# Output projection of attention in three fp32r terms, with wo split once and loaded from ScalarE's queue, and x in natural layout in other buffers

## The chip, the cores and the metric

The kernel runs on one core of a Trainium2 chip. The metric is the device time of one execution in microseconds (us). The kernel before took 2135.66 us as the median of three runs (2130.54 to 2139.39).

## The reference

The input x has 4 batches of 1024 tokens of 512 numbers. One layer of attention with 16 heads of 32 is followed by a mixture of experts; each adds its input and normalises. All is fp32. The change touches only the last two lines of attention:

```
q, k, v = x @ wq.T + bq, x @ wk.T + bk, x @ wv.T + bv        # 16 heads of 32
probs = softmax(q @ k.T / sqrt(32));  ctx = probs @ v          # per head
attn = ctx @ wo.T + bo                                        # ctx: 1024 x 512 per batch
x2 = layernorm(x + attn)                                      # then the expert part reads x2
```

## The kernel before, in words

Every engine has its own instruction list, written out in the code, and the engines meet at semaphores. A list is strictly in order: an instruction that waits holds up all that stands behind it.

**Batches and groups.** Attention goes through the batches b = 0 to 3. A batch has G = 4 groups of HG = 4 heads, a group has two halves of 512 queries (HALF), and a half has 8 steps of 128 keys. So there are 16 steps (STEPS) a group and 64 a batch (`loc`), with 4 slots each. In a step TensorE makes the scores (L625) of the next step, ScalarE their exps into one of three buffers of probabilities (L776), TensorE multiplies with v (L636). GpSimd and VectorE add the probabilities of two steps ("fold", L539 and L888) into `acc`, and TensorE sums them over the keys into `ps_sum` ("row sums", L649). Beside this TensorE makes max products (L603) and the k and q projections of a group two further on (L577) in three terms of fp32r, where VectorE takes the maxima (L860). fp32r is the faster matmul type; a high part and a low part (the rest) of both factors, in three products, replace one fp32 product.

**The spread.** SyncE copies the projected `kq` into `kq_stack` by twelve DMAs of 256 KB for each group ("spread", L342), then a row of negated maxima (L350, four small writes).

**The inversion.** When a half is done, ScalarE evicts ctx and the sums (L784, L791). SyncE gathers the sums into `sum_few` (L361, four small DMAs, "gather"), VectorE takes the reciprocal (L877), SyncE writes it out and broadcasts it into `res` (L367, L371), and GpSimd multiplies ctx with it (L503, "normalise"). An eighth of ctx, 512 columns of one group, is called a ctx part here; there are 8.

**The tail of a batch.** TensorE makes eight v tiles of the next batch (L569; 4 x 3 fp32r matmuls each, low part of wv reloaded by L396 since `wv_lo` shares its place with `probs_mid`), evicted by VectorE with bv (L906). Then come eight output tiles (L666) of 128 tokens: four fp32 matmuls each of ctx with wo, which appear as two instructions each. wo sits in `acc`, loaded by SyncE when the last row sums are done (L410). VectorE adds x with bo (L916), takes mean and variance (L918 to L924), GpSimd makes scale and shift (L515, L518), ScalarE applies them (L795) and SyncE stores the tile (L421). x in natural layout is loaded into `probs_outer` (L413) behind the inversion, and GpSimd adds bo (L510). Four PSUM banks go round (TAIL_RING). The results lie in `res` and `probs_mid`; between them ScalarE makes the first exps of the next batch. In the last batch there are no v tiles, and half of wo is loaded ahead into `stage` (L404).

**The start.** x and the first weights are split into high and low parts, batch 0's k and q of group 0 are projected, wv is split (ScalarE L822, VectorE L937), then v tiles and max products alternate (`prologue`).

## Time and profile before

| | |
|---|---|
| median of three runs | 2135.66 us |
| the profiled execution | 2128.77 us |
| its span | 2127.0 us |
| mean granted clock of TensorE | 0.99 of full speed |
| TensorE busy | 2040.6 us, 96% of the span |
| VectorE busy | 1266.4 us, 60% |
| ScalarE busy | 862.4 us, 41% |
| GpSimd busy | 871.3 us, 41% |

A busy share is an average over stages. Which engine sets the time of a stage is read from its waits: an engine that idles before an instruction has a releaser, named behind `<-`. Matmuls overlap, so the distance of their starts counts and not their duration. SyncE's rows show the time of issue, not of transfer. The inner tails lie at about 356 to 407, 672 to 723 and 988 to 1039 us, the last one at 1277 to 1315 us; what comes after is the expert part.

### The profile page before, as it was taken

The numbers are of one execution on the slowest core, as the hardware profiler recorded it, in microseconds if no ns is written. First come the engines' busy times: TensorE is split into PE (matmuls) and PEld (weight loads), VectorE is DVE, ScalarE is ACT, GpSimd is POOL, SyncE is SP. The second block draws the span as 40 slices with busy tenths as digits, with TensorE's granted clock in tenths as the row PEclk, the third lists the DMA queues.
The fourth block names the chain that finished last, engine by engine and source line by source line (L and its number), as shares of the span: only waits on it lengthen the run. The fifth ranks groups of instructions, "written<-read, shape, count | busy, mean of one in ns | idle before, by whom it ended". The sixth has DMA issues, their size and how long they took to land. (4 is left out here: it accounts for less than half of the span.)

```text
span 2127.0 us, 29932 instructions
## 1 busy us (share of the span) xinstructions
PE 2040.6 (96%) x9636; PEld 1202.1 (57%) x9637; DVE 1266.4 (60%) x2247; ACT 862.4 (41%) x1530; POOL 871.3 (41%) x828
## 2 busy tenths in 40 slices
PE   7999999999999999999999986899999999999997
PEld 5655556555556555556455432578544444446886
DVE  5777775577775677875678843574222222225875
ACT  2266663366663466663466661321111111112332
POOL 2255754455754555753555553400111111114651
PEclk9999999999999999999999998899999999999999
DMA  5322334221434231434231204661222222225752
GB/s 168 70 49 58 96 76 119 85 56 50 101 75 116 84 69 41 103 71 118 82 76 27 66 12 152 215 242 60 89 89 89 89 89 89 89 79 157 227 176 75
DMA packets 94815, 205.90 MB, mean 97 GB/s; under 512 B 24608, under 2 KB 25120, under 8 KB 92256
## 3 DMA queue, kind: packets, MB, share of 16 engines
q1 hardware_dynamic: 83888, 168.90, 27.1%
q0 software_dynamic: 10800, 35.40, 6.1%
q8 instruction: 69, 1.13, 0.2%
q14 instruction: 58, 0.48, 0.1%
HBM read 113.53 MB, written 39.85 MB: 72 GB/s over the span
## 5 line engine op out<-in xcount | busy, mean ns | idle before, releaser
L860 DVE TENSOR_REDUCE max_half<-ps_side 128x1 f32<-128x512 f32 x1024 | 657.9, 682 | 196.2 <-PE ps_side L603 193.4
L776 ACT ACTIVATE probs_outer<-ps_s 128x512 f32<-128x512 f32 x629 | 363.4, 600 | 210.4 <-PE ps_s L625 179.9
L603 PE MATMUL ps_side<-kq_stack 96*128 96x512 f32 x1024 | 409.2, 404 | 3.1 <-DVE max_half L860 2.3
L625 PE MATMUL ps_s<-kq_stack 97*128 97x512 f32 x937 | 397.1, 425 | 5.0 <-ACT probs_outer L776 3.3
L625 PEld LDWEIGHTS ps_s<-kq_stack 97*128 97x128 f32 x937 | 177.4, 189 | 167.1 <-issue 89.1
L1524 PE MATMUL ps_gu<-gu_sb,xT_e 128*128 x568 | 257.7, 596 | 0.7 <-issue 0.5
L1422 POOL DMA_INDIRECT x_g<-x,who_all x71 | 67.5, 951 | 454.7 <-PE ps_t L1514 358.4
L603 PEld LDWEIGHTS ps_side<-kq_stack 96*128 96x128 f32 x1024 | 195.0, 190 | 56.2 <-DVE max_half L860 26.6
L776 ACT ACTIVATE probs_mid<-ps_s 128x512 f32<-128x512 f32 x308 | 177.6, 599 | 116.0 <-PE ps_s L625 101.7
L539 POOL TENSOR_TENSOR acc<-probs_outer,probs_mid 128x512 f32<-128x512 f32 x129 | 163.9, 1296 | 144.7 <-ACT probs_mid L776 144.7
L539 POOL TENSOR_TENSOR acc<-probs_outer 128x512 f32<-128x512 f32 x129 | 163.4, 1291 | 125.6 <-ACT probs_outer L776 125.6
L539 POOL TENSOR_TENSOR acc<-probs_mid,probs_outer 128x512 f32<-128x512 f32 x118 | 149.7, 1293 | 120.7 <-ACT probs_outer L776 120.7
L636 PE MATMUL ps_ctx<-probs_outer,v_sb 128*32 128x512 f32 x1376 | 173.4, 599 | 0.5 <-ACT probs_outer L776 0.5
L1645 ACT ACTIVATE act_g<-ps_gu 128x256 f32<-128x256 f32 x71 | 27.3, 384 | 346.8 <-PE ps_gu L1524 346.8
L1524 PEld LDWEIGHTS ps_gu<-gu_sb,xT_e 128*128 128x128 f32 x568 | 102.3, 190 | 106.5 <-issue 106.2
L1722 DVE TENSOR_TENSOR hid<-act_g,ps_gu 128x256 f32<-128x256 f32 x71 | 29.9, 421 | 221.8 <-ACT act_g L1645 221.8
L649 PE MATMUL ps_sum<-acc,ones 128*32 128x512 f32 x1024 | 133.8, 594 | 11.2 <-DVE acc L888 7.1
L1547 PE MATMUL ps_d<-wd_sb,act_g 128*128 x284 | 133.7, 593 | 0.5 <-DVE act_g L1729 0.5
L577 PE MATMUL ps_side<-x_hi,wkq_hi 128*128 128x512 f32 x256 | 102.7, 401 | 12.3 <-DVE x_lo L931 10.7
L1466 PE MATMUL ps_gu<-sgu_hi,xT_hi 128*128 128x512 f32 x256 | 104.0, 406 | 3.0 <-issue 1.5
L1735 DVE COPY y_t<-ps_d 128x512 f32<-128x512 f32 x71 | 49.1, 692 | 93.4 <-PE ps_d L1547 93.4
L577 PE MATMUL ps_side<-x_lo,wkq_hi 128*128 128x512 f32 x256 | 102.2, 399 | 0.0
(210 smaller groups left out, 3055.2 us busy)
## 6 DMA issues: line engine op xcount, KB each, us to landing
kq_stack<-kq SPq DMA_DIRECT2D x192, 256.0 KB, 5.1
...
res<-inv_rows SPq DMA_DIRECT2D x128, 64.0 KB, 2.0
...
```

What stands on the lines that cost most here:

```text
L539: nc.gpsimd.tensor_tensor(acc[:, h, :], probs(loc - 1, h), probs(loc, h), ALU.add).then_inc(folded, 1)
L577: done = nc.tensor.matmul(bank, w, xs, start=r == 0, stop=r == UNIT - 1)
L603: nc.tensor.matmul(bank, q_stack[par][0:3 * HD, h, t * P:(t + 1) * P], k_stack[par][0:3 * HD, h, half * HALF:(half + 1) * HALF], start=Tru ...
L625: nc.tensor.matmul(out, k_stack[par][0:3 * HD + 1, h, kt * P:(kt + 1) * P], q_stack[par][0:3 * HD + 1, h, half * HALF:(half + 1) * HALF], ...
L636: done = nc.tensor.matmul(ps_ctx[h * HD:(h + 1) * HD, :], v_sb[:, kt, (g * HG + h) * HD:(g * HG + h + 1) * HD], probs(loc, h), start=kt == ...
L649: done = nc.tensor.matmul(ps_sum[h * HD:(h + 1) * HD, :], ones[:], acc[:, h, :], start=kt == FOLD - 1, stop=kt == KT - 1)
L776: nc.scalar.activation(probs(loc, h), score_bank(b, loc * HG + h)[0], ACT.Exp, scale=HD ** -0.5).then_inc(probs_ready, 1)
L860: nc.vector.reduce_max(max_half[:, u // 2, u % 2:u % 2 + 1], bank, AX.X).then_inc(side_free, 1)
L1422: nc.gpsimd.indirect_dma_start(x_g[:, t % 4, :], None, x2, bass.IndirectOffsetOnAxis(ap=who_all[:, t:t + 1].bitcast(U32), axis=0),).then_i ...
L1466: done = nc.tensor.matmul(out, w, m, start=c == 0 and i == 0, stop=c == last_c and i == 2)
L1524: done = nc.tensor.matmul(ps_gu[:, s % 2, :], e_xT[:, s % 2, c, :], gu_sb[:, bass.ds(e, 1), c, :].rearrange("p a n -> p (a n)"), start=c = ...
L1547: done = nc.tensor.matmul(ps_d[:, s % 2, :], e_hT[:, s % 2, c, :], wd_sb[:, bass.ds(e, 1), c, :].rearrange("p a n -> p (a n)"), start=c == ...
```

## The change

**The projection.** An output tile is made of 12 fp32r matmuls: high and low part of ctx with the high part of wo, and the high part of ctx with the low part of wo (new L714 to L717). The high part of ctx is written over `kq`, the low part over ctx itself. ScalarE makes the high parts (`ctx_high`, new L847), VectorE the low ones (`ctx_low`, new L976). Seven of the eight must be there for the first output tile, the eighth for the fifth. In the inner tails ScalarE makes them after the batch, once the spread has landed, and VectorE between its evictions of v; in the last batch seven are made inside the last group.

**wo.** It is loaded once at the start into `acc`, split by GpSimd and kept in DRAM as two halves of 1 MB. In each inner tail ScalarE's queue loads both (new L892) as soon as the row sums are done: into `acc` and into the third buffer of probabilities. In the last batch SyncE loads them in the middle of the batch over `x_hi` and `x_lo`.

**x.** Tiles 0 to 3 are loaded into the first buffer of probabilities, 4 and 5 into `stage`, both ahead of the inversion, 6 and 7 into `res` behind the last normalisation. The results of tiles 0 to 3 lie in `probs_mid`, the others take x's place. GpSimd adds bo to two tiles ahead of the last normalisation. The gather is a function of its own (`few`) and stands in the tail ahead of these loads.

**The start.** TensorE's first v tile waits for wv's low parts one by one, not for all four, and GpSimd waits for all of them before it splits its weights.

```diff
-NORM_AFTER, SPLIT_W_AFTER = (15, 9), 13
+NORM_AFTER, NORM_AFTER_LAST, SPLIT_W_AFTER = (15, 9), 11, 13
+CTX_ORDER = ((0, 0), (1, 0), (2, 0), (0, 1), (1, 1), (2, 1), (3, 0), (3, 1))
+CTX_HIGH_LAST = {10: (0, 1, 2), 12: (3, 4, 5), 14: (6,)}
+CTX_LOW_AFTER_V = {4: (0, 1, 2), 5: (3, 4), 6: (5, 6)}
...
+    wo_kept = nc.dram_tensor("wo_kept", (2, P, C, D), F32, kind="Internal").ap()
...
-        with nc.sbuf_tensor("probs_mid", [P, HG, HALF], F32) as probs_mid:
-            pass
-        wv_lo = sb("wv_lo", [P, C, D], F32R)
-        acc = sb("acc", [P, HG, HALF])
-        wo = acc
+        probs_mid, wv_lo = twin("probs_mid", "wv_lo", [P, HG, HALF])
+        acc, wo_hi = twin("acc", "wo_hi", [P, HG, HALF])
...
         v_sb = sb("v_sb", [P, KT, D])
-        probs_outer = sb("probs_outer", [P, 2, HG, HALF])
+        probs_first = sb("probs_first", [P, HG, HALF])
+        probs_last, wo_lo = twin("probs_last", "wo_lo", [P, HG, HALF])
...
 
-            return probs_mid[:, h, :] if loc % PROBS == 1 else probs_outer[:, loc % PROBS // 2, h, :]
...
+            return (probs_first, probs_mid, probs_last)[loc % PROBS][:, h, :]
+
+        ctx_sb, ctx_lo = twin("ctx_sb", "ctx_lo", [P, G, S])
+        ctx_hi = kq
+        first_wo = [ctx_lo[:, 2 * i:2 * i + 2, :].rearrange("p g (a d) -> p (g a) d", d=D) for i in range(2)]
...
+        def x_of(t):
+
+            return probs_first[:, t, :] if t < 4 else stage[:, t - 4, :] if t < 6 else res[:, t - 6, :]
+
         def res_of(t):
 
-            return probs_mid[:, t - 2, :] if 2 <= t < 6 else res[:, t % 2, :]
+            return probs_mid[:, t, :] if t < 4 else x_of(t)
...
                 if last and g == 1:
-                    sp.wait_ge(w_split, 2 * B * G)
-                    sp.dma_start(stage[:], woT[:, 0:2, :]).then_inc(wo_in, 16)
+                    sp.wait_ge(proj_ready, PROJ * B * G)
+                    sp.sem_inc(passed_sp, 1)
+                    for i, part in enumerate((x_hi, x_lo)):
+                        sp.dma_start(part[:, :, 0:D].bitcast(F32), wo_kept[i]).then_inc(wo_in, 16)
+
+            def load_x_nat(b, i, to):
+                sp.dma_start(to, x[bass.ds(b, 1), 2 * i * P:(2 * i + 2) * P, :].rearrange(
+                    "a (t p) d -> p (a t) d", p=P)).then_inc(xnat_in[i], 16)
 
             def tail(b, last=False):
+                few((b + 1) * G * NHALF - 1)
                 sp.wait_ge(sum_done, (b + 1) * SUMS)
                 sp.sem_inc(passed_sp, 1)
-                first = 2 if last else 0
-                sp.dma_start(wo[:, first:C, :], woT[:, first:C, :]).then_inc(wo_in, 16)
+                for i in range(2):
+                    load_x_nat(b, i, probs_first[:, 2 * i:2 * i + 2, :])
+                sp.wait_ge(w_split, 2 * min(b * G + G + 3, B * G))
+                load_x_nat(b, 2, stage[:])
                 invert((b + 1) * G * NHALF - 1)
-                for i in range(KT // 2):
-                    sp.dma_start(x_nat[:, 2 * i:2 * i + 2, :],
-                                 x[bass.ds(b, 1), 2 * i * P:(2 * i + 2) * P, :].rearrange(
-                                     "a (t p) d -> p (a t) d", p=P)).then_inc(xnat_in[i], 16)
+                sp.wait_ge(ctx_done, (b + 1) * G * NHALF)
+                load_x_nat(b, 3, res[:])
...
+            sp.dma_start(acc[:], woT).then_inc(const_in, 16)
...
-            sp.wait_ge(wv_split, C)
+            sp.wait_ge(part_low, C)
             sp.dma_start(wv_lo_kept, wv_lo[:].bitcast(F32)).then_inc(wv_moved, 16)
+            sp.wait_ge(const_set, WO_MADE)
+            for i in range(2):
+                sp.dma_start(wo_kept[i], first_wo[i].bitcast(F32)).then_inc(wv_moved, 16)
...
+            sp.wait_ge(wv_moved, KEPT)
...
+            pool.wait_ge(part_low, C)
...
             nc.gpsimd.tensor_copy(wkq_hi[:], first_w(1)).then_inc(w_high, 2)
             pool.wait_ge(w_high, 4)
             nc.gpsimd.tensor_tensor(wkq_lo[:], first_w(1), wkq_hi[:].bitcast(F32), ALU.subtract).then_inc(w_split, 2)
+            pool.wait_ge(const_in, CONSTS)
+            pool.wait_ge(w_split, 4)
+            nc.gpsimd.tensor_copy(first_wo[0], acc[:]).then_inc(const_set, 1)
+            pool.wait_ge(const_set, WO_MADE - 1)
+            nc.gpsimd.tensor_tensor(first_wo[1], acc[:], first_wo[0].bitcast(F32), ALU.subtract).then_inc(const_set, 1)
...
-                    if at == NORM_AFTER[0]:
+                    if at == (NORM_AFTER_LAST if last and g == G - 1 else NORM_AFTER[0]):
                         normalise(b, g, 0)
                     if at == SPLIT_W_AFTER and not (last and g > 0):
                         projected(b * G + g + 2)
                         split_w(b * G + g + 3)
                     if (g, at) in X_AFTER and not last:
                         x_low(b + 1, X_AFTER[g, at])
+                add_bo(b, 0)
+                add_bo(b, 1)
                 normalise(b, G - 1, 1)
-                add_bo(b)
+                for t in range(2, KT + 1):
+                    if t < KT:
+                        add_bo(b, t)
+                    scale_and_shift(b, t - 2)
+                scale_and_shift(b, KT - 1)
...
-            def o_tile(u, t, bank, parts):
+            def o_tile(u, b, t, bank, hi, lo):
+                if t % (KT // NHALF) == 0:
+                    pe.wait_ge(part_low, C + b * CTX_PARTS + (CTX_PARTS - 1 if t == 0 else CTX_PARTS))
                 pe.wait_ge(tail_free, u - TAIL_RING + 1)
+                at = slice(t * P, (t + 1) * P)
                 for g in range(G):
-                    done = nc.tensor.matmul(bank, ctx_sb[:, g, t * P:(t + 1) * P], parts[g],
-                                            start=g == 0, stop=g == G - 1)
+                    nc.tensor.matmul(bank, ctx_hi[:, g, at], hi[g], start=g == 0, stop=False)
+                    nc.tensor.matmul(bank, ctx_lo[:, g, at], hi[g], start=False, stop=False)
+                for g in range(G):
+                    done = nc.tensor.matmul(bank, ctx_hi[:, g, at], lo[g], start=False, stop=g == G - 1)
                 done.then_inc(tail_ready, 1)
...
-            pe.wait_ge(wv_split, C)
             pe.wait_ge(const_set, 5)
             for t, c, what in prologue():
                 if what is None:
+                    if t == 0:
+                        pe.wait_ge(part_low, c + 1)
                     v_tile(t, t, ps_s[:, t % RING, :], RING, [c])
...
-                pe.wait_ge(wo_in, 16 * (b + 1))
+                pe.wait_ge(wo_in, 32 * (b + 1))
                 for t in range(KT):
-                    if t % (KT // NHALF) == 0:
-                        pe.wait_ge(ctx_done, (b + 1) * G * NHALF - (t == 0))
-                    o_tile(b * TAIL + 2 * KT + t, t, tail_bank(KT + t),
-                           [wo[:, g, :] for g in range(G)])
+                    o_tile(b * TAIL + 2 * KT + t, b, t, tail_bank(KT + t),
+                           [wo_hi[:, g, :] for g in range(G)], [wo_lo[:, g, :] for g in range(G)])
...
             for t in range(KT):
-                if t % (KT // NHALF) == 0:
-                    pe.wait_ge(ctx_done, (b + 1) * G * NHALF - (t == 0))
-                o_tile(b * TAIL + KT + t, t, tail_bank(t),
-                       [stage[:, 0, :], stage[:, 1, :], wo[:, 2, :], wo[:, 3, :]])
+                o_tile(b * TAIL + KT + t, b, t, tail_bank(t),
+                       [x_hi[:, g, 0:D] for g in range(G)], [x_lo[:, g, 0:D] for g in range(G)])
...
+                    act.wait_ge(x2_out[h], 16 * (b + 1))
...
+            def ctx_high(b, i):
+                g, half = CTX_ORDER[i]
+                if i == 0:
+                    for s in stacked:
+                        act.wait_ge(s, SPREAD * min(b * G + G + 2, B * G))
+                act.wait_ge(ctx_done, b * CTX_PARTS + g * NHALF + half + 1)
+                at = (slice(None), g, slice(half * HALF, (half + 1) * HALF))
+                nc.scalar.activation(ctx_hi[at], ctx_sb[at], ACT.Copy).then_inc(part_high, 1)
...
+                    for i in CTX_HIGH_LAST.get(loc % STEPS, ()) if last and g == G - 1 else ():
+                        ctx_high(b, i)
...
+                act.wait_ge(wv_moved, KEPT)
+                act.wait_ge(sum_done, (b + 1) * SUMS)
+                for i, part in enumerate((wo_hi, wo_lo)):
+                    nc.scalar.dma_start(part[:].bitcast(F32), wo_kept[i]).then_inc(wo_in, 16)
+                for i in range(CTX_PARTS):
+                    ctx_high(b, i)
                 for t in range(KT):
                     norm(b, t)
...
             batch(B - 1, True)
+            ctx_high(B - 1, CTX_PARTS - 1)
             for t in range(KT):
...
+                    for i in CTX_HIGH_LAST.get(loc % STEPS, ()) if last and g == G - 1 else ():
+                        ctx_low(b, i)
+
+            def ctx_low(b, i):
+                g, half = CTX_ORDER[i]
+                at = (slice(None), g, slice(half * HALF, (half + 1) * HALF))
+                dve.wait_ge(part_high, C + b * CTX_PARTS + i + 1)
+                nc.vector.tensor_tensor(ctx_lo[at], ctx_sb[at], ctx_hi[at].bitcast(F32),
+                                        ALU.subtract).then_inc(part_low, 1)
...
                     v_tile(b * TAIL + KT + t, t, tail_bank(t))
                     if t == 2:
                         invert((b + 1) * G * NHALF - 1)
+                    for i in CTX_LOW_AFTER_V.get(t, ()):
+                        ctx_low(b, i)
                 for t in range(KT):
                     o_tile(b * TAIL + 2 * KT + t, b, t, tail_bank(KT + t))
+                    if t == 1:
+                        ctx_low(b, CTX_PARTS - 1)
```

VectorE in an inner tail, before. `max_row` is the last row of maxima, `v_sb` the eviction of a v tile, `inv_few` the reciprocal, the last row the eviction of the first output tile:

```order
L871 CAST max_row<-ps_side 16x128 [waits row_in1,side_ready]
L906 TENSOR_TENSOR v_sb<-ps_side,bv_bc 128x512 [waits tail_ready] x3
L877 RECIPROCAL inv_few<-sum_few 128x16 [waits rows_out,few_in]
L906 TENSOR_TENSOR v_sb<-ps_side,bv_bc 128x512 [waits tail_ready] x5
L916 TENSOR_TENSOR res<-ps_side,probs_outer 128x512 [waits xbias,tail_ready]
```

The same place now:

```order
L936 CAST max_row<-ps_side 16x128 [waits row_in1,side_ready]
L981 TENSOR_TENSOR v_sb<-ps_side,bv_bc 128x512 [waits tail_ready] x3
L942 RECIPROCAL inv_few<-sum_few 128x16 [waits rows_out,few_in]
L981 TENSOR_TENSOR v_sb<-ps_side,bv_bc 128x512 [waits tail_ready] x2
L976 TENSOR_TENSOR ctx_lo<-ctx_sb,kq 128x512 [waits part_high] x3
L981 TENSOR_TENSOR v_sb<-ps_side,bv_bc 128x512 [waits tail_ready]
L976 TENSOR_TENSOR ctx_lo<-ctx_sb,kq 128x512 [waits part_high] x2
L981 TENSOR_TENSOR v_sb<-ps_side,bv_bc 128x512 [waits tail_ready]
L976 TENSOR_TENSOR ctx_lo<-ctx_sb,kq 128x512 [waits part_high] x2
L981 TENSOR_TENSOR v_sb<-ps_side,bv_bc 128x512 [waits tail_ready]
L987 TENSOR_TENSOR probs_mid<-ps_side,probs_first 128x512 [waits xbias,tail_ready]
```

Seven low parts of ctx stand between the reciprocal and the first output tile, in and around the last v evictions.

SyncE's queue in an inner tail, before, from the last two rows of the spread; `kq_stack<-max_row` is the row write, `sum_few` the gather:

```order
L342 DMA kq_stack<-kq 32x2x1024 [waits scores_ready]
L342 DMA kq_stack<-kq 32x2x1024 x2
L350 DMA kq_stack<-max_row 1x4x128 [waits side_free]
L350 DMA kq_stack<-max_row 1x4x128 x3
L410 DMA acc<-woT 128x2048 [waits sum_done]
L361 DMA sum_few<-res 32x1x16 [waits sum_taken]
L361 DMA sum_few<-res 32x1x16 x3
L367 DMA inv_rows<-inv_few 128x16 [waits inverted,ctx_done]
L371 DMA res<-inv_rows 32x512 [waits rows_out]
L371 DMA res<-inv_rows 32x512 x3
L413 DMA probs_outer<-x 128x2x512 x4
```

The same place now:

```order
L363 DMA kq_stack<-kq 32x2x1024 x2
L371 DMA kq_stack<-max_row 1x4x128 [waits side_free]
L371 DMA kq_stack<-max_row 1x4x128 x3
L382 DMA sum_few<-res 32x1x16 [waits sum_taken]
L382 DMA sum_few<-res 32x1x16 x3
L434 DMA probs_first<-x 128x2x512 [waits sum_done]
L434 DMA probs_first<-x 128x2x512
L434 DMA stage<-x 128x2x512 [waits w_split]
L390 DMA inv_rows<-inv_few 128x16 [waits inverted,ctx_done]
L394 DMA res<-inv_rows 32x512 [waits rows_out]
L394 DMA res<-inv_rows 32x512 x3
L434 DMA res<-x 128x2x512 [waits ctx_done]
```

The load of wo is gone from this queue, and three loads of x stand ahead of the inversion's second half.

VectorE in the last group of the last batch now. `acc` is a fold; before, the same folds followed each other without the rows of `ctx_lo`:

```order
L954 TENSOR_TENSOR acc<-probs_last,probs_first 128x512 [waits sum_done,probs_ready]
L954 TENSOR_TENSOR acc<-probs_last,probs_first 128x512 [waits probs_ready]
L976 TENSOR_TENSOR ctx_lo<-ctx_sb,kq 128x512 [waits part_high] x3
L954 TENSOR_TENSOR acc<-probs_mid,probs_last 128x512 [waits sum_done,probs_ready]
L954 TENSOR_TENSOR acc<-probs_mid,probs_last 128x512 [waits probs_ready]
L976 TENSOR_TENSOR ctx_lo<-ctx_sb,kq 128x512 [waits part_high] x3
L954 TENSOR_TENSOR acc<-probs_first,probs_mid 128x512 [waits sum_done,probs_ready]
L954 TENSOR_TENSOR acc<-probs_first,probs_mid 128x512 [waits probs_ready]
L976 TENSOR_TENSOR ctx_lo<-ctx_sb,kq 128x512 [waits part_high]
L954 TENSOR_TENSOR acc<-probs_last,probs_first 128x512 [waits sum_done,probs_ready]
L954 TENSOR_TENSOR acc<-probs_last,probs_first 128x512 [waits probs_ready]
L942 RECIPROCAL inv_few<-sum_few 128x16 [waits rows_out,few_in]
```

Three low parts stand ahead of a pair of folds twice, and one a third time.

## Rows read from the trace of the kernel before

**Rows 1.** Timeline of TensorE, tails of batches 0, 1: start, us, line, tile, [idle<-releaser]

```profile
354.53 1.06 PE L649 MATMUL ps_sum<-acc,ones 128*32 128x512 f32 x8 [0.18 <-DVE acc L888]
...
359.04 0.39 PE L569 MATMUL ps_side<-wv_hi,x_hi 128*128 128x512 f32 x1
...
377.17 0.39 PE L569 MATMUL ps_side<-wv_lo,x_hi 128*128 128x512 f32 x1
...
378.08 17.33 PE L666 MATMUL ps_side<-acc,ctx_sb 128*128 128x512 f32 x40
...
694.04 17.33 PE L666 MATMUL ps_side<-acc,ctx_sb 128*128 128x512 f32 x40
```

**Rows 2.** Timeline of TensorE, last batch's last group and tail

```profile
1258.84 1.06 PE L649 MATMUL ps_sum<-acc,ones 128*32 128x512 f32 x8 [2.20 <-issue]
...
1281.43 3.55 PE L666 MATMUL ps_side<-stage,ctx_sb 128*128 128x512 f32 x4 [3.90 <-DMA acc<-woT]
...
1284.81 1.88 PE L666 MATMUL ps_side<-acc,ctx_sb 128*128 128x512 f32 x4
...
1308.85 1.88 PE L666 MATMUL ps_side<-acc,ctx_sb 128*128 128x512 f32 x4
```

**Rows 3.** Timeline of VectorE: reciprocals in tail 0, in a body, in tail 1

```profile
372.91 0.25 DVE L877 RECIPROCAL inv_few<-sum_few 128x16 f32<-128x16 f32 x1 [7.54 <-DMA sum_few<-res]
...
444.74 0.25 DVE L877 RECIPROCAL inv_few<-sum_few 128x16 f32<-128x16 f32 x1 [0.17 <-DMA sum_few<-res]
...
690.14 0.25 DVE L877 RECIPROCAL inv_few<-sum_few 128x16 f32<-128x16 f32 x1 [8.81 <-DMA sum_few<-res]
```

**Rows 4.** Timeline of SyncE's queue (SPq): us is the time of issue

```profile
25.41 14.10 SPq L342 DMA_DIRECT2D kq_stack<-kq  x12
...
349.39 14.28 SPq L342 DMA_DIRECT2D kq_stack<-kq  x12
...
363.71 3.41 SPq L350 DMA_DIRECT2D kq_stack<-max_row  x4
...
367.65 2.50 SPq L361 DMA_DIRECT2D sum_few<-res  x4
...
441.19 2.42 SPq L361 DMA_DIRECT2D sum_few<-res  x4
...
684.16 2.49 SPq L361 DMA_DIRECT2D sum_few<-res  x4
```

**Rows 5.** Timeline of TensorE at the start

```profile
28.09 0.50 PE L569 MATMUL ps_s<-wv_hi,x_hi 128*128 128x512 f32 x1 [4.29 <-DVE wv_lo L937]
...
35.27 0.40 PE L603 MATMUL ps_side<-kq_stack 96*128 96x512 f32 x1
```

**Rows 6.** Timeline of ScalarE at the start

```profile
8.56 4.25 ACT L816 ACTIVATE x_hi<-probs_outer 128x512 fp32r<-128x512 f32 x8
```

**Rows 7.** Timeline of VectorE: start, last group, last tail

```profile
9.91 4.89 DVE L931 TENSOR_TENSOR x_lo<-probs_outer,x_hi 128x512 fp32r<-128x512 f32 x8
...
25.22 2.81 DVE L937 TENSOR_TENSOR wv_lo<-ctx_sb,wv_hi 128x512 fp32r<-128x512 f32 x1
...
1261.97 2.60 DVE L888 TENSOR_TENSOR acc<-probs_mid,probs_outer 128x512 f32<-128x512 f32 x2 [3.24 <-ACT probs_outer L776]
...
1303.89 0.69 DVE L916 TENSOR_TENSOR probs_mid<-ps_side,probs_outer 128x512 f32<-128x512 f32 x1 [1.48 <-PE ps_side L666]
```

**Rows 8.** Timeline of GpSimd: start, last group, last tail

```profile
25.15 2.34 POOL L525 TENSOR_TENSOR wkq_lo<-ctx_sb,wkq_hi 128x1024 fp32r<-128x1024 f32 x1 [0.15 <-POOL wkq_hi L523]
...
1261.04 2.97 POOL L539 TENSOR_TENSOR acc<-probs_mid,probs_outer 128x512 f32<-128x512 f32 x2 [3.46 <-ACT probs_outer L776]
...
1287.54 1.27 POOL L503 TENSOR_TENSOR ctx_sb<-ctx_sb,res 128x512 f32<-128x512 f32 x1 [10.09 <-DMA res<-inv_rows]
```

**Rows 9.** Windows of tail 0: busy us per engine, TensorE clock, DMA share, GB/s

```profile
356.00:360.00 4.00, 3.82 (x17) 3.17 (x18) 0.81 (x2) 0.25 (x1) 0.00 (x0) 1.00 1.04 223
...
380.00:384.00 4.00, 4.00 (x10) 1.71 (x9) 1.18 (x2) 0.00 (x0) 3.02 (x3) 1.00 1.01 364
```

81 lines of the change are left out of this document (44 added, 37 removed).

## The prediction

> **What bounds the kernel now.** I read the page's engine shares first (TensorE is busy nearly all of the span), then the timeline of each engine around the four output projections, then SyncE's queue and the DMA share there. Only attention changes; the expert part behind it shifts as a block, so what counts is when TensorE finishes the last output tile. The reader should see three things.
>
> Between batches TensorE runs without a gap: eight v tiles in fp32r, a matmul every 0.2266 us (18.13 us for the 80 between the L569 rows of [rows 1]; 12 make a tile, 2.72 us), and behind them the output tiles in fp32, two instructions per matmul, 3.43 us a tile (24.04 us for seven tiles in [rows 2]). So in the three inner tails TensorE's own work is the path.
>
> Inside that cover VectorE is already late. Its order has the reciprocal behind the third v tile, and it waits there for the small gather of sums: 7.54 us in batch 0 [rows 3]. That gather stands in SyncE's queue behind the twelve 256 KB copies of the spread (14.28 us), four row writes (3.41 us) and the 1 MB load of wo, whose issue is the gap to 367.65 [rows 4]. The reciprocal of batch 0 is 5.17 us ahead of the first output tile, batch 1's 3.90 us. Nothing but five v evictions follows it today, so it just fits.
>
> The last batch waits 3.90 us for wo [rows 2]. The start waits 4.29 us for the last low part of wv, and then runs slowly: 24 matmuls in 7.18 us instead of 5.44 [rows 5].
>
> **The change, part by part.** *Matmuls.* The new output tile has the shape and dtype of the v tile: 12 matmuls at 0.2266, 2.72 us, against 3.43. That is 0.714 us a tile. In the inner tails 24 tiles give 17.1 us, if they start on time.
>
> *The splits ahead of the tile.* Seven of eight ctx parts need a high part (ScalarE) and a low part (VectorE) before the first output tile. ScalarE has been idle since the batch's end; it makes eight such parts in 4.25 us [rows 6], and they are off the path. VectorE's order is now: reciprocal, v, v, three lows, v, two lows, v, two lows. With 0.61 us each (eight in 4.89, as x_lo at the start; a v eviction takes the same) the eleven make 6.7 us. GpSimd adds bo to two x tiles in that time, and its two-input work slows VectorE's two-input work: two folds took 2.60 us, 1.3 each, beside it [rows 7, 8]. For 2.6 us of overlap I add 1.5 and 0.2 for the reciprocal and hand-offs: 8.4 us from reciprocal to first output tile. Against 5.17 and 3.90 that alone is 3.2 us of stall in batch 0, 4.5 in batch 1, and 4.5 in batch 2 as well.
>
> *When the reciprocal comes.* With wo's load gone from SyncE's queue the gather is issued 0.5 us earlier, and lands behind nothing: in the body the reciprocal follows the last gather's issue by 1.13 us (444.74 against 443.61), in batch 0's tail by 2.76, in batch 1's by 3.49 [rows 3, 4]. Gain, with some 0.1 lost again: 2.0 us in batch 0, 2.7 in the others. Against it, ScalarE issues 2 MB (wo high and low) as soon as the last row sums are done, at 355.6 [rows 1], when half the spread is still to be issued. In 356 to 360 the DMA share is 1.04 at 223 GB/s; the x load in 380 to 384 has 1.01 at 364 GB/s [rows 9]. So the engines have no room, and 2.10 MB at 364 GB/s are 5.8 us of them. Bounds for the delay of spread, row writes and gather: nothing, if the slow spread leaves gaps that wo fills, and 9.4 us, if wo moves at the spread's 223 GB/s in its place. Full engines speak for the upper half, the low rate at a full share for some slack; I take 5.8 x 223/364 = 3.5 us.
>
> The Trainium skill (DMA: Bandwidth & Descriptors, "Issuing engines are not separate DMA queues") says that DMAs from ScalarE and SyncE end up on the same engines and interleave, and that another issuing engine saves issue time alone. By that rule the whole 5.8 us is delay and the total below becomes 4.9 us slower instead of 2.0 faster. Whether the trace agrees can't be said: no row shows two hardware queues at once.
>
> *Sum of the inner tails.* Stalls (3.2 - 2.0) + 2 x (4.5 - 2.7) = 4.8, plus 3 x 3.5 = 15.3 us. TensorE then stands idle some 4 us before the first output tile, and after idle times of 3.90 and 4.29 us it ran slowly: the first four instructions took 3.38 us instead of 1.72 [rows 2], 24 matmuls 7.18 instead of 5.44 [rows 5]; after 2.20 us it had no such slow stretch [rows 2]. 1.6 us each, 4.9 in all. Inner tails: 15.3 + 4.9 - 17.1 = +3.1 us.
>
> *Start.* Two edits meet. TensorE's first v tile now waits for wv's low parts one by one, and GpSimd waits for all four before it splits wkq. Today its subtraction (25.15, 2.34 us) lies on VectorE's last low part, which took 2.81 us where a low part of x takes 0.61 [rows 7, 8]. So TensorE goes on from 23.8 (28.09 - 4.29) with three parts and has the fourth at 25.9; without idle time it keeps its rate, and both first tiles end at about 29.4 instead of 35.3 [rows 5]. Then the first max product waits for head 0 of the spread: three of twelve copies, issued from 25.41, 3.5 us of 14.10 [rows 4], and some 2 us to land: 31.2. Bounds 29.4 and 35.3. Behind it VectorE's maxima are the path, so the start gains 4.1 us. The new split of wo (1 MB load, a cast and a subtraction of 2048 columns, two 1 MB writes) falls where GpSimd and the DMA engines idle until the next weights; by 2.34 us for 1024 columns it is some 7 us of GpSimd. Its first reader behind that cover is the first fold, 60 us later: nothing.
>
> *Last batch.* Seven parts are split inside its last group, where the loop is bound by exps, folds and row sums. Three lows stand ahead of VectorE's folds twice, one a third time. Two at 1.3 (GpSimd folds and normalises beside them) and one at 0.7, less the idle time they fill, I put at 2.7, 2.2 and 1.2: +6.1 us. Bounds: 0 (all in today's idle time of 3.2 us a pair), and 9 (all seven at 1.3). Then the tail: today 33.2 us from the row sums' end (1281.43 - 3.90) to the last tile's end at 1310.7 [rows 2]. Afterwards the gate is the last ctx part. Its normalisation starts 10.0 us behind the sums (1287.54, [rows 8]); with 1.5 MB of x ahead of the broadcast in the same queue, partly under the inversion, I take 11.4. Then 1.3 for it, 0.7 and 0.8 for its parts, four tiles at 2.72, and 1.6 for the slow restart: 26.7 us, 6.5 less. That makes 6.1 - 6.5 = -0.4; since the wait before the fifth tile is only some 3.4 us, between 2.20 and 3.90, I spare 0.6 of the restart: -1.0 us.
>
> *x in other places, exps.* x tiles 0 to 5 now load before the inversion, so VectorE's wait for bias-added x goes; TensorE didn't wait for it, with four banks. The next batch's exps wait for stores 0 to 3 instead of 2 to 5, which are earlier. Both nothing. SyncE's 2 MB load in the last batch stands ahead of a gather that VectorE reads only at slot 24 of the next group's 64; 5.8 us fit.
>
> *Total.* +3.1 - 4.1 - 1.0 = -2.0 us. The profiled execution took 2128.77 us (span 2127.0), which is 6.9 below the median of the runs, 2135.66; it becomes 2126.8, and the median 2133.7.
>
> **The rivals.** With d as the delay of the spread, the total is 3d - 12.5 us with three slow restarts.
>
> A. The two queues share well, d = 0. For: spread packets run at 61% of the x load's rate, so something other than the engines may hold them. Against: the share of 1.04. Stalls are 4.8 us, TensorE idles under 2 us and doesn't slow down: 4.8 - 17.1 - 4.1 - 1.0 = -17.4, median 2118.3.
>
> B. The other side: wo takes the spread's place at the spread's rate, d = 9.4, in the three inner tails; the gather comes after everything, and VectorE begins its eleven steps when TensorE has long run dry. 3 x 9.4 - 12.5 = +15.7, median 2151.4. It loses to before from d = 4.2, and by more than 0.5% from d = 7.7. For: the four row writes already take 3.41 us behind the spread, so SyncE's issue is held by what is queued. Against: wo's own 1 MB moved at over 223 GB/s today.
>
> C. The three terms don't pay, because VectorE or the weight loads set the output tiles' pace. Then 17.1 us are missing: +15.1, median 2150.8. Against: of 3.43 us VectorE idles 1.48 before each result [rows 7], so its work is 1.95, under 2.72, and the v tiles with the same matmuls keep 0.2266.
>
> **How the numbers follow.** Forecast 0.52, A 0.29, B 0.13, C 0.04, the rest 0.02. What tells from no change here is 0.5%, 10.7 us. The forecast's own range, d from 2 to 6, the step of 8.4 us off by 1 and the last group's bounds, is 2125 to 2143. For 8 in 10 it reaches into A and B: 2117 to 2147. Faster by over 0.5% (below 2125.0): most of A and an edge of the forecast, 0.31. Slower (above 2146.3): B, C, little else, 0.15. Within: 0.54.
>
> **What would show it.** Right: output tiles 2.72 us apart; the reciprocal of batch 0 some 1.5 us later behind the row sums (today 17.3); the seven lows between it and the first output tile, and TensorE idle 3 to 5 us there, released by VectorE; a slow stretch after it; the first v matmul at about 24 us, and the first max product near 31; row sums of the last group 2 us later twice. Wrong: the spread still takes 14.3 us with wo beside it (A), or over 22 (B); the idle time before the output tiles under 1 us, or ended by a DMA; output tiles over 3 us apart (C); a last group that isn't longer.

## The result, and the profile after

| | before | after |
|---|---|---|
| median (three runs before, four after) | 2135.66 us | 2158.22 us (2154.66 to 2159.1) |
| profiled span | 2127.0 us | 2156.4 us |
| mean granted clock | 0.990 | 0.981 |

The ratio is 1.0106, 95% interval 1.0087 to 1.0124: slower, where I had forecast 2133.7 us and a range up to 2147. The spans differ by 29.4 us and the medians by 22.6, because the profiled execution of before, 2128.77 us, lies 6.9 under its median; the stages below are read from the spans. S is the end of a batch's last row sums on TensorE, and a tail runs from S to the end of its last output tile.

| stage | before | after | difference | forecast |
|---|---|---|---|---|
| start to S of batch 0 | 355.6 | 352.4 | -3.2 | -4.1 |
| inner tails | 51.1, 51.1, 51.4 | 60.9, 60.1, 59.3 | +26.7 | +3.1 |
| bodies of batches 1, 2 | 264.9, 264.8 | 267.0, 266.1 | +3.4 | 0 |
| body of batch 3, with the last group | 238.7 | 244.4 | +5.7 | +6.1 |
| last tail | 33.2 | 30.1 | -3.1 | -7.1 |
| behind it | 816.3 | 816.2 | -0.1 | 0 |

Nearly all of the miss lies in the inner tails. The timeline of TensorE in the kernel after, tail 0, then where output tiles start in tails 1 and 2 (these answer to [rows 1]; columns as there):

```profile
351.31 1.06 PE L694 MATMUL ps_sum<-acc,ones 128*32 128x512 f32 x8 [0.19 <-DVE acc L954]
355.58 0.76 PE L614 MATMUL ps_side<-wv_hi,x_hi 128*128 128x512 f32 x1 [2.99 <-issue]
378.33 0.50 PE L614 MATMUL ps_side<-wv_hi,x_hi 128*128 128x512 f32 x1 [2.01 <-DVE v_sb L981]
387.88 0.76 PE L714 MATMUL ps_side<-wo_hi,kq 128*128 128x512 f32 x1 [4.95 <-issue]
392.99 0.39 PE L714 MATMUL ps_side<-wo_hi,kq 128*128 128x512 f32 x1
395.74 0.39 PE L714 MATMUL ps_side<-wo_hi,kq 128*128 128x512 f32 x1
...
714.48 0.77 PE L714 MATMUL ps_side<-wo_hi,kq 128*128 128x512 f32 x1 [4.11 <-issue]
1040.72 0.77 PE L714 MATMUL ps_side<-wo_hi,kq 128*128 128x512 f32 x1 [5.14 <-issue]
```

The tiles themselves do what they should: 392.99 to 395.74 is one tile, 2.75 us. But the first comes 35.5 us after S (352.37), where it came at 22.5. TensorE stops on the way in the middle of the v tiles and again ahead of the output tiles, in all three tails, and the first output tile takes 5.11 us (387.88 to 392.99) at the lower clock (granted 0.50 in 388 to 392). The stop of 2.99 us ahead of the v tiles is in tail 0 alone. It also comes in kernels without an early load of wo (1.68 us in E2, 2.26 in E6), and it is not on the path here, since the output tiles wait for the reciprocal and what follows it.

The reciprocals on VectorE in tails 0, 1 and 2, with low parts of tail 0 (they answer to [rows 3]), and GpSimd beside them:

```profile
377.48 0.25 DVE L942 RECIPROCAL inv_few<-sum_few 128x16 f32<-128x16 f32 x1 [11.31 <-DMA sum_few<-res]
378.79 3.39 DVE L976 TENSOR_TENSOR ctx_lo<-ctx_sb,kq 128x512 fp32r<-128x512 f32 x3
384.51 3.28 DVE L976 TENSOR_TENSOR ctx_lo<-ctx_sb,kq 128x512 fp32r<-128x512 f32 x2
...
704.03 0.25 DVE L942 RECIPROCAL inv_few<-sum_few 128x16 f32<-128x16 f32 x1 [14.00 <-DMA sum_few<-res]
1030.12 0.25 DVE L942 RECIPROCAL inv_few<-sum_few 128x16 f32<-128x16 f32 x1 [13.93 <-DMA sum_few<-res]
```

```profile
378.05 2.98 POOL L545 TENSOR_TENSOR probs_first<-probs_first,bo_bc 128x512 f32<-128x512 f32 x2 [25.74 <-DMA probs_first<-x]
384.31 1.26 POOL L541 TENSOR_TENSOR ctx_sb<-ctx_sb,res 128x512 f32<-128x512 f32 x1 [3.28 <-DMA res<-inv_rows]
385.53 1.71 POOL L545 TENSOR_TENSOR probs_first<-probs_first,bo_bc 128x512 f32<-128x512 f32 x1
```

The first three low parts took 1.13 us each, beside GpSimd's two additions of bo, and the last two 1.64 each, beside its normalisation and a third addition. The reciprocals come 25.1, 23.8 and 23.7 us after S, where they came at 17.3, 18.6 and 19.1. What holds the gather stands in SyncE's queue and ScalarE's (the rows that answer to [rows 4]), and in the landing times of the DMAs from 352.4 to 378.4:

```profile
346.16 12.23 SPq L363 DMA_DIRECT2D kq_stack<-kq  x12
358.43 2.55 SPq L371 DMA_DIRECT2D kq_stack<-max_row  x4
361.03 2.64 SPq L382 DMA_DIRECT2D sum_few<-res  x4
363.79 3.38 SPq L434 DMA_DIRECT2D probs_first<-x  x2
352.50 0.36 ACTq L892 DMA_DIRECT2D wo_hi<-wo_kept  x1
352.88 1.21 ACTq L892 DMA_DIRECT2D wo_lo<-wo_kept  x1
```

```profile
kq_stack<-kq SPq DMA_DIRECT2D x8, 256.0 KB, 14.6
wo_hi<-wo_kept ACTq DMA_DIRECT2D x1, 1024.0 KB, 12.3
wo_lo<-wo_kept ACTq DMA_DIRECT2D x1, 1024.0 KB, 18.5
sum_few<-res SPq DMA_DIRECT2D x4, 2.0 KB, 12.2
```

The spread in the kernel before (352.4 to 378.4 us there):

```profile
kq_stack<-kq SPq DMA_DIRECT2D x9, 256.0 KB, 7.5
```

The last column is the median time from issue to landing. The spread is issued even faster than before (12.23 us against 14.28), so the sign that I had named, spread rows over 22 us, does not appear. It lands later: 14.6 us from its issue instead of 7.5. The gather is issued at 361 and lands 12.2 us later. The windows of the same tail (they answer to [rows 9]) show full DMA engines up to 374, at 200 to 289 GB/s:

```profile
354.00:358.00 4.00, 2.42 (x6) 1.97 (x7) 0.00 (x0) 0.00 (x0) 0.00 (x0) 0.66 1.03 200
358.00:362.00 4.00, 4.00 (x18) 3.25 (x17) 0.69 (x1) 0.00 (x0) 0.00 (x0) 0.92 1.01 289
362.00:366.00 4.00, 4.00 (x20) 3.30 (x19) 1.21 (x2) 0.00 (x0) 0.00 (x0) 1.00 1.02 287
366.00:370.00 4.00, 4.00 (x19) 3.34 (x18) 0.18 (x1) 0.00 (x0) 0.00 (x0) 1.00 1.04 220
370.00:374.00 4.00, 4.00 (x19) 3.30 (x19) 0.00 (x0) 0.00 (x0) 0.00 (x0) 1.00 1.04 232
```

The last batch on TensorE (row sums of its last group, then the fifth output tile, which answer to [rows 2]), and GpSimd's last normalisation ([rows 8]):

```profile
1285.60 1.07 PE L694 MATMUL ps_sum<-acc,ones 128*32 128x512 f32 x8 [2.19 <-issue]
1294.56 1.06 PE L694 MATMUL ps_sum<-acc,ones 128*32 128x512 f32 x8 [2.46 <-DVE acc L954]
1302.40 1.07 PE L694 MATMUL ps_sum<-acc,ones 128*32 128x512 f32 x8 [2.82 <-DVE acc L954]
1309.02 1.07 PE L694 MATMUL ps_sum<-acc,ones 128*32 128x512 f32 x8 [1.90 <-DVE acc L954]
1326.85 0.80 PE L714 MATMUL ps_side<-x_hi,kq 128*128 128x512 f32 x1 [5.66 <-DVE ctx_lo L976]
```

```profile
1323.76 1.26 POOL L541 TENSOR_TENSOR ctx_sb<-ctx_sb,res 128x512 f32<-128x512 f32 x1 [4.19 <-DMA res<-inv_rows]
```

The start: the first max product, the high part of the next projection on ScalarE, and the first score matmul:

```profile
31.05 0.50 PE L648 MATMUL ps_side<-kq_stack 96*128 96x512 f32 x1 [1.73 <-DMA kq_stack<-kq]
82.52 1.19 PE L670 MATMUL ps_s<-kq_stack 97*128 97x512 f32 x2
```

```profile
43.64 0.69 ACT L792 ACTIVATE kq<-ps_side,bkq 128x512 fp32r<-128x512 f32 x1 [18.95 <-DMA kq_stack<-kq]
```

### The profile page after: what moved, and what is told of

The parts are those of the page before. It is cut to its first block and busy times, and to the rows that moved or that the text cites. A ratio compares the mean times of both kernels' runs of the same rounds, so it can differ in the third digit from the quotient of the medians.

```text
span 2156.4 us, 30282 instructions
## 1 busy us (share of the span) xinstructions
PE 2035.2 (94%) x9764; PEld 1234.1 (57%) x9765; DVE 1294.8 (60%) x2279; ACT 879.4 (41%) x1562; POOL 880.3 (41%) x830
## 3 DMA queue, kind: packets, MB, share of 16 engines
q1 hardware_dynamic: 84656, 169.95, 26.9%
## 5 line engine op out<-in xcount | busy, mean ns | idle before, releaser
L823 ACT ACTIVATE probs_first<-ps_s 128x512 f32<-128x512 f32 x326 | 187.4, 599 | 108.8 <-PE ps_s L670 93.8
L578 POOL TENSOR_TENSOR acc<-probs_first,probs_mid 128x512 f32<-128x512 f32 x129 | 163.4, 1291 | 148.5 <-ACT probs_mid L823 148.5
L823 ACT ACTIVATE probs_last<-ps_s 128x512 f32<-128x512 f32 x303 | 175.5, 599 | 98.8 <-PE ps_s L670 83.3
L578 POOL TENSOR_TENSOR acc<-probs_last,probs_first 128x512 f32<-128x512 f32 x129 | 163.0, 1289 | 128.8 <-ACT probs_first L823 128.8
L578 POOL TENSOR_TENSOR acc<-probs_mid,probs_last 128x512 f32<-128x512 f32 x118 | 149.3, 1290 | 119.6 <-ACT probs_last L823 119.6
L694 PE MATMUL ps_sum<-acc,ones 128*32 128x512 f32 x1024 | 133.8, 594 | 17.6 <-DVE acc L954 13.7
```

Source lines behind the costliest of these rows:

```text
L578: nc.gpsimd.tensor_tensor(acc[:, h, :], probs(loc - 1, h), probs(loc, h), ALU.add).then_inc(folded, 1)
L694: done = nc.tensor.matmul(ps_sum[h * HD:(h + 1) * HD, :], ones[:], acc[:, h, :], start=kt == FOLD - 1, stop=kt == KT - 1)
L823: nc.scalar.activation(probs(loc, h), score_bank(b, loc * HG + h)[0], ACT.Exp, scale=HD ** -0.5).then_inc(probs_ready, 1)
```

## The experiments

Twelve kernels, each timed beside the kernel before; every ratio is to before, from the same chip. "Rec" is the time from S to the reciprocal in the three inner tails.

### Where wo's load stands: E1, E2, E4, E9

E1 moves the two loads from ScalarE's queue to SyncE's, behind the gather:

```
 # SyncE, tail
+if not last:
+    for i, part in enumerate((wo_hi, wo_lo)):
+        sp.dma_start(part[:].bitcast(F32), wo_kept[i]).then_inc(wo_in, 16)
 for i in range(2): load_x_nat(...)
```

> Edit: the two 1 MB loads of wo go from ScalarE's queue to SyncE's, behind the gather of sums and ahead of x; all else is the changed kernel. Theory T (the 2.10 MB of wo share the engines with the spread, so the gather, which waits behind the spread's packets, lands 9.4 us later than it would alone): the reciprocal comes 15 to 16 us after the last row sums instead of 25.1 (377.48 - 352.37 in batch 0), VectorE's eleven steps end 24 to 26 us after them, and the first output tile starts there instead of 35.5, 34.3 and 34.3 us after. TensorE's two idle times of each tail (2.0 and 4.95; 4.70 and 4.11; 4.63 and 5.14) become one of 1 to 3.5. Some 9 to 10 us less a tail, -27 to -30 us: 2130 us. Rival X (the 1.57 MB of x that now stand ahead of the inversion delay it): the reciprocal stays 23 us or more behind the row sums, 2150 to 2160 us. Rival V (VectorE's steps are the limit in any case): the reciprocal comes early, and the first output tile still starts more than 30 us after the row sums, 2145 us.

2125.35 us, ratio 0.9965 (0.9952 to 0.9977) where the changed kernel has 1.0106: faster than before. Rec is 15.1, 15.4 and 15.4 us. The first output tile starts 22.5 us after S in all three, without a gap, which is better than expected: from reciprocal to output tile it took 7.1 to 7.4 us, because x lands behind the low parts and GpSimd's additions (at 378.00 in tail 0) no longer meet them. So E1 removes two costs at once, and the 13.0 us that tail 0 gains at its first output tile are not the gather's alone. The first row is VectorE's, the second TensorE's, and the others are DMAs with their landing times:

```profile
370.19 0.25 DVE L943 RECIPROCAL inv_few<-sum_few 128x16 f32<-128x16 f32 x1 [5.33 <-DMA sum_few<-res]
```

```profile
377.57 0.39 PE L717 MATMUL ps_side<-wo_hi,kq 128*128 128x512 f32 x1
```

```profile
kq_stack<-kq SPq DMA_DIRECT2D x7, 256.0 KB, 7.5
wo_hi<-wo_kept SPq DMA_DIRECT2D x1, 1024.0 KB, 4.9
sum_few<-res SPq DMA_DIRECT2D x4, 2.0 KB, 2.2
```

The gather lands in 2.2 us instead of 12.2, and behind it wo and x move at a rate that they never reached beside the spread (window 371 to 375 of E1: share 0.96 at 397 GB/s):

```profile
371.00:375.00 4.00, 4.00 (x19) 3.34 (x18) 4.00 (x7) 1.99 (x4) 0.00 (x0) 1.00 0.96 397
```

E2 leaves the loads in ScalarE's queue and only makes them wait: `act.wait_ge(few_in, 16 * HG * (b + 1) * G * NHALF)` ahead of them.

> Edit: the two loads of wo stay in ScalarE's queue, but ScalarE first waits for the last gather of sums to land. It tells the moment of issue from the queue. T: only the moment counts, since the two queues share the same engines: the reciprocal 15 to 16 us behind the row sums as in the version with wo behind the gather in SyncE's queue; wo's 2.10 MB and x's 1.57 MB then move together, 10.1 us at 364 GB/s, so wo lands about 26 us after the row sums, at the end of the v tiles (22 us) or up to 4 us past it: 2128 to 2140 us. If a second queue were a loss of its own: the reciprocal over 20 us, 2150 us.

2131.62 us, ratio 0.9993 (0.9982 to 1.0003). Rec is 15.4, 15.6 and 15.3: the moment counts, not the queue. Here x shares the engines with wo, and wo lands late, 26 to 27 us after S, as the first output tile of tail 0 shows:

```profile
380.98 0.50 PE L714 MATMUL ps_side<-wo_hi,kq 128*128 128x512 f32 x1 [3.17 <-DMA wo_lo<-wo_kept]
```

E4 loads one megabyte instead of two from ScalarE's queue: it leaves out the low half of wo and uses the high half in its place.

> Edit: in the three inner tails only the high half of wo is loaded (1.05 MB), and its product with the low half uses it once more in place of the low half. A dose test. T: the delay goes with the bytes, 9.4 us for two megabytes at the spread's 223 GB/s: reciprocal 4.7 us earlier, 20.4 behind the row sums instead of 25.1, each inner tail 4 to 5 us shorter, -12 to -14 us: 2145 us. If the delay is a fixed cost of a second queue: the reciprocal stays above 23, 2155 us.

2147.24 us, ratio 1.0066 (1.0045 to 1.0088). Rec is 19.2, 18.7 and 19.7. So from none (E1) over one to two megabytes the means are 15.3, 19.2 and 24.2 us: the delay goes with the bytes. E10 below loads as the changed kernel does and has 22.9.

E9 issues wo from SyncE's queue behind the spread and ahead of the gather.

> Base: the changed kernel (2158.22 us, reciprocal 23.7 to 25.1 us behind the row sums of the three inner tails; 15.1 to 15.4 with wo behind the gather). Edit: wo's 2 MB are issued at about the same moment, but from SyncE's queue, right behind the spread and ahead of the gather. It tells 'beside the spread in a second queue' from 'ahead of the gather'. If bytes ahead are all that counts and they move at the 364 GB/s of large loads once the spread is through, 5.8 us: reciprocal at 21, 2145 to 2148 us. If two queues at once are what makes it slow, the same or less: 20 or 21 with TensorE's idle time 3 us less. If wo's bytes always move at the spread's 223 GB/s, 9.4 us: reciprocal at 24 to 25, 2155 to 2160 us.

2146.05 us, ratio 1.0073 (1.0049 to 1.0096). Rec is 20.2, 20.4 and 20.6 us, 5.1 more than in E1. That is near the 5.8 us of two megabytes at the rate of large loads, the first of the three expectations, and rules out the third. The second allowed this reciprocal too, but TensorE's idle time did not shrink (6.72 us before the output tiles of tail 0), since VectorE's steps still took 10.5 us.

### What x and bo cost: E3, E10

E3 loads x tiles 0 to 5 behind the inversion, and normalises ahead of both additions of bo:

```
+invert((b + 1) * G * NHALF - 1)
 for i in range(2): load_x_nat(...)
...
 load_x_nat(b, 2, stage[:])
-invert((b + 1) * G * NHALF - 1)
```

> Edit: x tiles 0 to 5 load behind the inversion again, and GpSimd adds bo to the first two after it normalises; wo's loads stay as in the changed kernel. T: the gather is no earlier (reciprocal still 24 to 26 us behind the row sums in the three inner tails); only the inversion's own write, which took 5.4 us to land in the last tail behind 1.57 MB of x and 3.0 in batch 0, lands in some 1.5 us, and VectorE's lows no longer meet the addition of bo. Last tail -3 us, inner tails -1 to -2 each: 2150 to 2155 us. Rival X: x ahead of the inversion is what holds the gather, reciprocal at 16 us: 2130 us.

2145.97 us, ratio 1.0066 (1.0049 to 1.0084), 4 us better than the best that I expected. Rec is 22.0, 21.7 and 22.5 us, 2.1 less in the mean than in the changed kernel, though x stood behind the gather there. How much of this is x's is not settled: E10 below has x in the old place and comes at 24.1, 22.7 and 22.1, only 0.9 more than E3 in the mean. Reciprocal to first output tile took 7.7, 7.7 and 6.9 us instead of 10.4 to 10.6. The last tail became longer, 31.8 us, because its evictions wait for x.

E10 moves the two additions of bo alone:

```
-add_bo(b, 0)
-add_bo(b, 1)
 normalise(b, G - 1, 1)
+add_bo(b, 0)
+add_bo(b, 1)
```

> Base: the changed kernel (2158.22 us). Edit: GpSimd adds bo to the first two x tiles behind its last normalisation instead of ahead of it; all loads stay. In the changed kernel VectorE's first three lows took 1.13 us each beside those additions instead of 0.6, and reciprocal to first output tile took 10.40 to 10.60 us, where I had 8.4. Theory: GpSimd's additions are the 2 us and more: 7.5 to 8.5 us from reciprocal to first output tile, each inner tail 2 to 3 us shorter; the last tail 1 to 2 us longer, since its evictions wait for bo: 2150 to 2153 us. Rival: the wait for ScalarE's high parts or the last normalisation sets it, and it stays over 10: 2158.

2144.24 us, ratio 1.0058 (1.0038 to 1.0078), 6 us better than the best that I expected. Reciprocal to first output tile is 6.90, 6.90 and 6.91 us, 3.5 less, and the three lows take 0.63 us each. The normalisation now starts at 387.54, behind all seven, so the last two are as quick:

```profile
380.39 0.26 DVE L942 RECIPROCAL inv_few<-sum_few 128x16 f32<-128x16 f32 x1 [14.09 <-DMA sum_few<-res]
381.70 1.89 DVE L976 TENSOR_TENSOR ctx_lo<-ctx_sb,kq 128x512 fp32r<-128x512 f32 x3
```

```profile
387.29 0.47 PE L714 MATMUL ps_side<-wo_hi,kq 128*128 128x512 f32 x1 [1.13 <-issue]
```

The last tail paid 4.1 us (34.2), twice the upper end of what I expected. The inner tails are 6.8 to 7.5 us shorter each: 3.5 to 3.7 by the steps, 1.9 to 2.8 because the output tiles no longer start slowly, and 1.0 to 1.6 because the reciprocal is earlier (24.1, 22.7 and 22.1 us after S). The last part I can't explain by the edit, since the loads are the same; profiled executions with the same loads can differ by that much.

### The last batch: E5, E6, E7

All three stand on E1. E5 splits the ctx parts one by one behind the folds:

```
-CTX_HIGH_LAST = {10: (0, 1, 2), 12: (3, 4, 5), 14: (6,)}
+CTX_HIGH_LAST = {3: (0,), 5: (1,), 7: (2,), 9: (3,), 11: (4,), 13: (5, 6)}
```

> Base: the version with wo behind the gather (2125.35 us). Edit: in the last batch's last group the seven ctx parts are no longer split in blocks of three, three and one ahead of the folds, but one by one behind a pair's folds (two behind the last but one). Theory L: the group's three long pairs (row sums 8.96, 7.84 and 6.62 us apart in the changed kernel, 5.87, 5.90 and 5.85 before) come from where the parts stand: ScalarE's high parts sit between exps and VectorE's low parts ahead of the folds that TensorE waits for, while VectorE idles 3.2 us a pair. Behind the folds they fit: all row sums 5.9 to 6.2 apart, -4.5 to -5.8 us: 2119 to 2121. Rival W: it is the work itself (seven high parts of 0.55 and seven low parts of 0.65 to 1.1 us beside GpSimd's folds), and it costs as much wherever it stands: 2124 to 2126.

2117.79 us, ratio 0.9926 (0.9909 to 0.9942). The row sums of the group on TensorE are 6.61, 5.88 and 5.86 us apart, so it was the place and not the work (the 0.7 us left in the first pair is no more than E7 shows there without any split, 6.95 us):

```profile
1256.86 1.06 PE L697 MATMUL ps_sum<-acc,ones 128*32 128x512 f32 x8
1262.74 1.07 PE L697 MATMUL ps_sum<-acc,ones 128*32 128x512 f32 x8 [0.86 <-DVE acc L955]
1268.60 1.07 PE L697 MATMUL ps_sum<-acc,ones 128*32 128x512 f32 x8 [1.15 <-DVE acc L955]
```

E6 puts the last tail's inversion between the first and the second load of x.

> Base: the version with wo behind the gather (2125.35 us). Edit: in the last tail only, the first 0.5 MB of x loads ahead of the inversion, the other 1.05 MB of tiles 2 to 5 behind it. There the inversion's own 8 KB write took 5.4 us to land behind 1.57 MB of x in the same queue, and the last ctx part was normalised 13.7 us behind the row sums instead of 10.0; TensorE idled 5.66 us before its fifth tile and then ran slowly. Theory: with 0.5 MB ahead the write lands 2.5 to 3.5 us sooner, the idle time falls to 2 or 3 us, and the slow stretch may go too (2 us): 2120 to 2123 us. Rival: VectorE's eviction of the first tiles, which wait for x plus bo, ends the wait in any case: 2125.

2121.4 us, ratio 0.9946 (0.9927 to 0.9965), an interval that overlaps E1's; the gain is read from the tail. In the profiled execution the batch's body took 3.6 us more than in E1, with pairs of 10.09 and 8.98 us, which I did not explain. The last tail takes 26.2 us instead of 30.0; the inversion's write lands in 2.4 us instead of 5.4, the part is normalised 10.7 us after S (1280.99), and TensorE idles 2.27 us. The slow stretch stays (window 1294 to 1298: clock 0.64). GpSimd's row and TensorE's:

```profile
1291.65 1.27 POOL L547 TENSOR_TENSOR ctx_sb<-ctx_sb,res 128x512 f32<-128x512 f32 x1 [1.04 <-DMA res<-inv_rows]
```

```profile
1294.36 0.50 PE L720 MATMUL ps_side<-x_hi,kq 128*128 128x512 f32 x1 [2.27 <-DVE ctx_lo L980]
```

E7 computes the last output projection in fp32 again, from wo loaded early in that batch.

> Base: the version with wo behind the gather (2125.35 us). Edit: the last batch's output projection goes back to fp32 (two instructions a matmul, 3.43 us a tile), without any split of ctx; wo as it stands (1.05 MB) loads early in that batch. It asks whether three terms pay there at all. Theory: the last group loses its 5.8 us of splits; the tail is 8 x 3.43 = 27.4 us plus 0 to 3 us of waits, against 29.07 now, because four fp32 tiles (13.7 us) cover the way of the last ctx part (13.4). -5 to -8 us: 2118 to 2120. Rival: the three terms save their 5.7 us there too, and the splits' price is not recovered: 2125 or more.

2119.95 us, ratio 0.9934 (0.9919 to 0.9948). Its tail takes 29.2 us (1272.29 to 1301.49), E1's 30.0, and the body with the last group 241.0 against 244.4. So as the change places the splits, three terms lose 4.2 us in the last batch by these stages (5.4 by the medians). Placed as in E5 and E6, which E8 joins, they win by the stages:

> Base: the version with wo behind the gather (2125.35 us), with both edits of the last batch: ctx parts split one by one behind the folds, and two thirds of x behind the inversion. If L and the inversion's queue place both hold, the gains add: 2115 to 2118 us. If one only hides behind the other: 2119 to 2122.

2113.99 us, ratio 0.9918 (0.9898 to 0.9937): the row sums are 5.88, 5.89 and 5.86 us apart, the body takes 238.6 us as before (238.7), and the tail 26.2 us, 3.0 less than in E7. Body and tail together are 5.3 us shorter than E7's; the intervals of the two whole times overlap.

### The start alone, and a version that beats both: E11, E12

E11 is the kernel before with the two waits of the start changed (TensorE's per low part, GpSimd's for all four).

> Base: the kernel before (2135.66 us). Edit: the start alone: TensorE waits for wv's low parts one by one and GpSimd for all of them before it splits wkq. In the changed kernel the first v matmul came at 23.29 and the first max product at 31.05 (28.09 and 35.27 before), but the first score matmul only at 82.52 (85.12), and in four other versions with the same start at 83.7 to 84.5: ScalarE's high part of the next projection waits for the whole spread to land, which is no earlier. Theory: first max product at 31 to 32, VectorE then idles 1.8 us near 44, first score matmul 1.0 to 2.6 us earlier: 2133 to 2135 us, same within what can be told. By my forecast of 4.1 us: 2131.5.

2127.62 us against 2129.46 for before on that chip, ratio 0.9992 (0.998 to 1.0004). First max product and first score matmul:

```profile
31.71 0.50 PE L604 MATMUL ps_side<-kq_stack 96*128 96x512 f32 x1 [1.85 <-DMA kq_stack<-kq]
83.23 0.86 PE L626 MATMUL ps_s<-kq_stack 97*128 97x512 f32 x2
```

The gain of 3.6 us at the first max product is 1.9 at the first score matmul (85.12 before). The whole time can't be told from no change.

E12 adds to E8's version `EXPS_BETWEEN = {2: ((0, 0), (0, 1)), ...` in place of `{3: ...`.

> Base: the version with both edits of the last batch and wo behind the gather (2113.99 us). Edit: the next batch's first two exps stand behind the third norm instead of the fourth on ScalarE. In the three inner tails TensorE idles 1.25 to 1.84 us before the third of the next batch's score matmuls, because those two exps wait behind a norm whose shift GpSimd makes late, while their scores are done 3 us earlier. Theory: that idle time goes, -1.2 to -1.8 us a tail, -4 us: 2110 us. Rival: the norm that is now behind them delays stores and the next exps by as much: 2114.

2102.97 us (2102.31 to 2103.68), ratio 0.987 (0.9852 to 0.9888). TensorE's idle time before the third score matmul is gone, and the inner tails take 46.2, 45.9 and 46.0 us against 51.1 to 51.4 before, and 47.4 to 47.9 in E8. It is the best version that I have: the changed kernel with its loads and splits in other places. By the ratios it gains some 10 us over E8's, by the profiled spans 5.8 (2107.7 to 2101.9), and the tails explain 4.8. Most of the difference between the two counts is that E8's profiled execution was the quickest of its five (2109.38 us against a median of 2113.99).

## Why the prediction was wrong

*The step that failed* is the one on the reciprocal: "Full engines speak for the upper half, the low rate at a full share for some slack; I take 5.8 x 223/364 = 3.5 us." There was no slack; the term was mis-sized. Between E1 and the changed kernel the reciprocal moves by 10.0, 8.4 and 8.3 us, 26.7 in place of my 10.5. (The gain from wo leaving SyncE's queue, E1 against before, was 9.1 us in sum where I had 7.4.) So the delay d of the formula was 8.9 us in the mean and not 3.5. Of this 6.8 are wo's in the second queue (E3 against E1). The other 2.1 are x behind the gather, or chance: E10, with the same loads, has 7.6 in all. I had x's early load down for nothing. By my own formula 8.9 gives +14.2 us, so rival B had the sign and nearly the size of d (9.4); its total, +15.7, still falls short of the measured 22.6, for the splits and the clock below. Its mechanism was nearly right too; only the sign to look for was wrong, the issue of the spread instead of its landing.

The inner tails missed by 23.6 us. The reciprocal makes 14.5 of them (26.7 - 9.1 in place of 10.5 - 7.4), the splits 6.3, the clock 2.1 and the matmuls 0.5.

The rule of the Trainium skill that I weighed (DMA: Bandwidth & Descriptors, "Issuing engines are not separate DMA queues") is borne out: E2 shows that it is the moment that counts and not the queue, and the 5.8 us that I had worked out by it stand between the 5.1 of E9 and the 6.8 of E3. Even so its total of 4.9 us slower would have been too low. I had it in hand and took the lower value because no row showed two queues at once; a full DMA share was the row.

*The splits.* 8.4 us from reciprocal to output tile were 10.4, 10.45 and 10.6, 6.3 us over my figure in sum. I charged 1.5 us for GpSimd's two additions, and the first three low parts took just that more (3.39 us against 1.89 in E10). The other 2.0 us fell on the last two (3.28 against 1.28), where the normalisation and a third addition stood: 5.9 us of GpSimd in all. The row of [rows 8] that I used for the last tail shows this normalisation, and I did not ask what it meets. E10 shows that without the two early additions the eleven steps take 6.9. GPSIMD Engine Reference of the Trainium skill (section 1, "Specifications") says that GpSimd's SBUF interfaces contend with VectorE's instructions that have two SBUF inputs; the trace agrees, 1.13 and 1.64 us a low part beside it and 0.63 without.

*The clock.* I had 1.6 us a tail for a slow restart; from first output tile to the end the three tails take 25.4, 25.9 and 25.0 us against 23.05 where TensorE did not slow down (E10, tails 1 and 2), so 1.9 to 2.8 each, 2.1 us more in sum. TensorE stopped twice ahead of the output tiles and not once, because the evictions of v tiles four and five stand behind the reciprocal; that cost nothing more, since the output tiles wait for VectorE anyway.

*The matmuls* were right: 28.57 us became 23.05 without a stall, 16.6 us in three tails against 17.1.

*The start* came out right up to the first max product (31.05 against 31.2), in part by luck: I gave the three copies of head 0 3.5 us to be issued and 2 to land, and they took 1.4 and 4.5 (26.49 to 31.00). Then it lost a third of its gain, 2.6 us being left at the first score matmul (82.52). In the other kernels with this start that matmul comes at 82.3 to 84.5 us and S of batch 0 at 350.5 to 356.3, so neither these 2.6 us nor the 3.2 at S are firm; E11 alone has 1.9. ScalarE's high part of the next projection overwrites what the spread reads, so it waits for all twelve copies to land, and these were no earlier (43.53 us against 43.16). I had asked what releases the maxima and not what releases the next step.

*The last batch.* The last group was right, 5.7 us against 6.1, with its first two pairs 3.1 and 1.9 us longer. The tail gained 3.1 and not 7.1: I had the normalisation at 11.4 us after the sums and it came at 13.7, because the inversion's 8 KB write took 5.4 us to land behind 1.57 MB of x. The wait before the fifth tile became 5.66 us in place of 3.4, and brought the slow restart that I had spared.

*The bodies* of batches 1 and 2 are 2.1 and 1.3 us longer, and those of the other versions vary by as much (264.8 to 268.8). In the changed kernel one fold in each of them (477.23 and 870.55) took 2.59 us; the first stood beside GpSimd's normalisation, where before (470.63) it met it for less time and took 1.35. I read this as chance of phase, and did not test it.
